# Four scheduling edits in an eight-image chain of attention layers: moments, q and k pieces, whole-width logits, and sums of the last tile on the tensor engine

## The reference

```python
def layer0(x):                       # channel attention
    q, k, v = split(W @ groupnorm32(x) + b)          # 8 heads
    a = softmax(q @ k.T * 32**-0.5)                  # 32 x 32 per head
    return x + P @ (a @ v) + pb
def layer1(x):                       # pixel attention, one head
    q, k, v = split(Wa @ x)                          # 32, 32, 128 channels
    return x + gamma * Wo @ (v @ softmax(q.T @ k).T) # 1024 x 1024
def layer2(x):                       # pixel attention, 8 heads
    q, k, v = split(W2 @ groupnorm8(x) + b2)
    return x + P2 @ (v @ softmax(q.T @ k * 32**-0.5).T) + pb2
def layer3(x):                       # the same, with the normalised x added
    n = groupnorm8(x); q, k, v = split(W3 @ n)
    return n + P3 @ (v @ softmax(q.T @ k * 32**-0.5).T) + pb3
```

## Time and profile before

| | us |
|---|---|
| median of 3 runs | 3036.81 |
| lowest, highest | 3025.49, 3037.48 |
| the profiled execution | 3033.91 |
| its span, first to last instruction | 3032.1 |

### The profile page before, as it was taken

The page is one execution under the profiler, slowest core; times in us unless marked ns, Lnnn a source line. Parts: engine busy times, 40 slices in busy tenths (PEclk is TensorE's granted clock), DMA queues, the critical chain, the costliest instruction groups (busy, mean ns, idle before and its releaser), DMA issues.

```text
span 3032.1 us, 36216 instructions
## 1 busy us (share of the span) xinstructions
PE 2834.0 (93%) x13152; PEld 1401.0 (46%) x13152; DVE 1858.0 (61%) x3293; ACT 1551.2 (51%) x2794; POOL 2178.6 (72%) x746
## 2 busy tenths in 40 slices
PE   7879999999999999999999999999999999999998
PEld 4444445544455444544445444454444544444442
DVE  1346665566756667566665666656675566767672
ACT  2214555445545555455564455544555445555554
POOL 3208787687767778677786778768777587798877
PEclk9879999999999999999999999999999999999999
DMA  2070343303433135233340334412343313433340
GB/s 83 19 95 16 44 72 58 51 19 44 85 44 54 33 46 90 31 44 57 44 86 13 43 58 71 58 28 32 54 72 58 46 23 44 72 45 44 44 58 15
DMA packets 74388, 150.87 MB, mean 50 GB/s; under 512 B 9121, under 2 KB 10657, under 8 KB 74210
## 3 DMA queue, kind: packets, MB, share of 16 engines
q1 hardware_dynamic: 74210, 148.56, 32.4%
HBM read 20.46 MB, written 16.78 MB: 12 GB/s over the span
## 4 chain that ended last, share of the span: by engine, by line
PE 63%; DMA 12%; ACT 8%; DVE 7%; POOL 6%; issue 3%; SPq 1%; ACTq 0%; POOLq 0%; DVEq 0%
PE psum L1308 15%; PE psum L1333 11%; PE psum L1277 10%; DMA Q<-lo 7%; PE psum L1252 5%; PE psum L1221 5%; PE psum L1229 4%; ACT prob L926 4%; POOL acc L822 3%; PE psum L1329 3%; DVE maxpart L1058 3%; DMA K<-hi 3%; POOL vT L822 2%; DMA Q<-max_rows 2%; PE psum L1154 2%
## 5 line engine op out<-in xcount | busy, mean ns | idle before, releaser
L1058 DVE TENSOR_REDUCE maxpart<-psum 128x1 f32<-128x512 f32 x2176 | 1411.7, 683 | 789.3 <-PE psum L1277 764.6
L926 ACT ACTIVATE prob<-psum 128x512 f32<-128x512 f32 x2176 | 1223.5, 596 | 935.0 <-PE psum L1308 888.1
L822 POOL TENSOR_TENSOR acc<-acc,prob 128x2048 f32<-128x2048 f32 (+1 forms) x322 | 1151.6, 3576 | 170.2 <-ACT prob L926 141.2
L1308 PE MATMUL psum<-Q,K 104*128 104x512 f32 x2048 | 1080.6, 529 | 94.3 <-ACT prob L926 73.5
L1277 PE MATMUL psum<-K,Q 96*128 96x512 f32 x2048 | 837.3, 411 | 32.1 <-DMA K<-hi 17.9
L1308 PEld LDWEIGHTS psum<-Q,K 104*128 104x128 f32 x2048 | 390.0, 191 | 798.8 <-ACT prob L926 487.3
L822 POOL TENSOR_TENSOR vT<-vT,prob 128x2048 f32<-128x2048 f32 x123 | 560.7, 4558 | 16.9 <-ACT prob L926 4.6
L1333 PE MATMUL psum<-prob,vT 128*32 128x512 f32 x4096 | 571.3, 618 | 0.0
L1277 PEld LDWEIGHTS psum<-K,Q 96*128 96x128 f32 x2048 | 398.3, 195 | 178.3 <-issue 89.3
L822 POOL TENSOR_TENSOR acc<-prob 128x2048 f32<-128x2048 f32 (+1 forms) x58 | 212.0, 3656 | 333.2 <-PE psum L1354 168.2
L1333 PEld LDWEIGHTS psum<-prob,vT 128*32 128x32 f32 x4096 | 99.8, 109 | 197.7 <-ACT prob L926 117.6
(11 more groups left out here) (138 smaller groups left out, 2129.2 us busy)
## 6 DMA issues: line engine op xcount, KB each, us to landing
Q<-hi SPq DMA_DIRECT2D x128, 256.0 KB
K<-hi SPq DMA_DIRECT2D x128, 256.0 KB
Q<-lo SPq DMA_DIRECT2D x64, 256.0 KB
K<-lo SPq DMA_DIRECT2D x64, 256.0 KB
scratch<-xa SPq DMA_DIRECT2D x8, 1024.0 KB, 4.0
xb<-scratch SPq DMA_DIRECT2D x8, 1024.0 KB, 4.9
xa<-in_x SPq DMA_DIRECT2D x7, 1024.0 KB, 8.4
out<-hb SPq DMA_DIRECT2D x7, 1024.0 KB, 5.7
```

Of the source, the lines that this page charges most:

```text
L822: pool.tensor_tensor(total, first if a == 1 else total, this, ALU.add).then_inc(added, 1)
L926: act.activation(prob[STEP_STARTS.slot(b, start)][:, j, :], score_bank[(SCORES.rank[b.n][e] - 1) % SCORE_BANKS], ACT.Exp, scale=1.0 if lay ...
L1058: dve.tensor_reduce(maxpart[layer][:, a // NQ, a % NQ:a % NQ + 1], bank, AX_X, ALU.max).then_inc(max_free, 1)
L1308: pe.matmul(score_bank[(r - 1) % SCORE_BANKS], left, right, start=True, stop=True).then_inc(score_full, 1)
```

## The change

Four edits.

1. "norm" loses its ACT part, which becomes an event of its own, ("moments", layer), two or three slots later. In most places "side mean" and "power" then move by one or two slots as well.
2. The q and k pieces of four heads come as q0, k0, k1, q1 where they came as q0, q1, k0, k1, at a fixed pace (every 5 slots for the early ones, every 4 for the late ones) where they were spread evenly (3.5 slots apart). The pair hi/lo is picked by (m + i) % 2, and a max product waits only for the stack that it reads. In the serial stretch of turn 0 the four v pieces are put between them.
3. The logits of four heads are one product 128 wide per half; only the blocks on the diagonal are used. DVE works on four blocks one by one, so that the maximum and the subtraction become four instructions each.
4. `pooled` takes the turn in which a group began: in turns 1 and 9, POOL leaves the last tile to PE in all groups.

```diff
-            + [("norm", layer), ("side", layer, "mean"), ("power", layer)]
+            + [("norm", layer), ("moments", layer), ("side", layer, "mean"), ("power", layer)]
...
+def place_operands(layer, t):
+    q, k = split_operand(layer, 2 * t), split_operand(layer, 2 * t + 1)
+    return q[:2] + k + q[2:]
...
+    def paced(first, step, pieces):
+        return at([first + step * i + c for i in range(len(pieces) // 2) for c in (0, 1, 1)], cut(pieces))
...
-            a += [(0, ("load",))] + at((10, 12, 14, 16, 17, 20, 23), normalise(0))
+            a += [(0, ("load",))] + at((10, 12, 14, 16, 17, 20, 22, 24), normalise(0))
...
-            a += at((1, 2, 3, 4, 5, 8, 11, 15, 16, 17, 18), normalise(3))
+            a += at((1, 2, 3, 4, 5, 8, 10, 12, 15, 16, 17, 18), normalise(3))
...
-                  + at((17, 17, 18, 18, 19, 23, 25, 28, 29, 30, 31), out1[T * NQ + 1:]),
+                  + at((17, 17, 18, 18, 19, 21, 23, 25, 28, 29, 30, 31), out1[T * NQ + 1:]),
...
-                 (3, 2, spread(1, 15, early2), [(3, 3, 8, 32, 0, 23), rows(3, 3, 27), (2, 0, 0, 8, 24, 31)]),
+                 (3, 2, paced(1, 5, early2), [(3, 3, 8, 32, 0, 23), rows(3, 3, 27), (2, 0, 0, 8, 24, 31)]),
...
-                 (2, 0, spread(0, 14, late2) + spread(SCALED, end, out3),
+                 (2, 0, paced(0, 4, late2) + spread(SCALED, end, out3),
...
-    return KC - 1 if layer != 2 and g > 0 or layer == LAST3 or (layer, g) == (2, 1) else KC
+    light = layer != 2 and g > 0 or layer == LAST3 or (layer, g) == (2, 1) or n in (1, B + 1)
+    return KC - 1 if light else KC
...
+    def split_home(m, i):
+        return (m + i) % 2
...
-                            act.wait_ge(stacked[i], b.until(STACKED[i], e))
+                            act.wait_ge(stacked[home], b.until(STACKED[home], e))
...
-                    elif e[0] == "norm":
-                        act.wait_ge(vstep, b.after(VSTEPS, e))
+                    elif e[0] == "moments":
+                        act.wait_ge(vstep, b.after(VSTEPS, ("norm", e[1])))
...
-                        own(dve.tensor_reduce(l0max[:, :], logits, AX_X, ALU.max))
+                        for r, logits in blocks:
+                            ins = dve.tensor_reduce(l0max[r, :], logits, AX_X, ALU.max)
+                        own(ins)
+                        for r, logits in blocks:
+                            ins = dve.tensor_tensor(l0[e[1]][r, :, :], logits,
+                                                    l0max[r, :].unsqueeze(2).broadcast_to([DH, T, DH]), ALU.subtract)
...
+                                ch = slice(t * P, (t + 1) * P)
+                                for k in range(T):
+                                    pe.matmul(side_bank[:, ch], wqk0_sb[:, k, ch], gk[layer][:, k, ch],
+                                              start=(k == 0), stop=False)
+                                ins = pe.matmul(side_bank[:, ch], rows0_sb[:, ch],
+                                                su_rows[layer][:, C + ch.start:C + ch.stop], start=False, stop=True)
...
-                        if a == 0 and (layer == 1 and g == 0 or layer != 1 and g % NQ == 0):
-                            ms = [0] if layer == 1 else [g // NQ * 2, g // NQ * 2 + 1]
-                            for i in range(2):
-                                pe.wait_ge(stacked[i], b.last(STACKED[i], [("stack", layer, m, i) for m in ms], e))
+                        elif g % NQ:
+                            first_use = [(m, 1)] if a == 0 else []
+                        else:
+                            first_use = {0: [(m, 0), (m + 1, 0)], 1: [(m + 1, 1)]}.get(a, [])
```

More of the change, by code:

```diff
@@ L131, in group_sequence @@
     out1 = after_layer1(False)
-    early2, late2 = (split_operand(2, m) + split_operand(2, m + 1) for m in (0, 2))
-    early3, late3 = (split_operand(3, m) + split_operand(3, m + 1) for m in (0, 2))
+    early2, late2 = (place_operands(2, t) for t in range(T))
+    early3, late3 = (place_operands(3, t) for t in range(T))
     rest0 = channel_attention(False)
@@ L170, in group_sequence @@
     early_halves, late_halves = (side(2, f"v{half}", KC // HPT) for half in range(T))
+    v2 = side(2, "v", KC // 2)
     maxima2 = [("max", 2, 0, a) for a in range(MAXIMA[2])]
@@ L441, in adds @@
         _, layer, g, s = e
+        began = n if ("score", layer, g, 0, 0) in PLANS[n][:i] else n - 1
         tiles = range(HPT * s, HPT * (s + 1)) if layer == 1 else [s]
-        return [("add", layer, g, a) for a in tiles if a and (layer == 1 or a < pooled(layer, g))]
-    ADDS = Events(PLANS, adds)
-    STACKED = [Events(PLANS, lambda e, s=s: [e] if e[0] == "stack" and e[-1] % 2 == s else [],
+        return [("add", layer, g, a) for a in tiles if a and (layer == 1 or a < pooled(began, layer, g))]
+    ADDED = [[adds(n, i, e) for i, e in enumerate(plan)] for n, plan in enumerate(PLANS)]
+    ADDS = Events([[x for of in turn for x in of] for turn in ADDED], lambda e: [e])
+    def split_home(m, i):
+        return (m + i) % 2
+    STACKED = [Events(PLANS, lambda e, s=s: [e] if e[0] == "stack" and split_home(*e[2:]) == s else [],
                       lambda e: 16 * (7 if e[1] == 1 else 3)) for s in range(2)]
@@ L695, in program @@
                         _, layer, m, i = e
-                        t, s, part = m // 2, m % 2, slice(i * QW, (i + 1) * QW)
+                        t, s, part, home = m // 2, m % 2, slice(i * QW, (i + 1) * QW), split_home(m, i)
                         low = b.after(PIECES, ("side", layer, "qk", m, i))
@@ L799, in program @@
                         slot, before = prob[VALUES.slot(b, e)], prob[VALUES.slot(b, e) - 1]
-                        for add in adds(e):
+                        for add in ADDED[b.n][b.place[e]]:
                             a = add[3]
@@ L1263, in program @@
                         half = slice((a % NQ) * QW, (a % NQ + 1) * QW)
-                        if a == 0 and (layer == 1 and g == 0 or layer != 1 and g % NQ == 0):
-                            ms = [0] if layer == 1 else [g // NQ * 2, g // NQ * 2 + 1]
-                            for i in range(2):
-                                pe.wait_ge(stacked[i], b.last(STACKED[i], [("stack", layer, m, i) for m in ms], e))
+                        m = 0 if layer == 1 else g // NQ * 2
+                        if layer == 1:
+                            first_use = [(0, a)] if g == 0 and a < NQ else []
+                        elif g % NQ:
+                            first_use = [(m, 1)] if a == 0 else []
+                        else:
+                            first_use = {0: [(m, 0), (m + 1, 0)], 1: [(m + 1, 1)]}.get(a, [])
+                        for piece in first_use:
+                            home = split_home(*piece)
+                            pe.wait_ge(stacked[home], b.last(STACKED[home], [("stack", layer) + piece], e))
                         if layer == 1:
@@ L1339, in program @@
                         _, layer, g = e
-                        add = ("add", layer, g, (KC if layer == 1 else pooled(layer, g)) - 1)
-                        at = ("values", layer, g, STEPS[1] - 1 if layer == 1 else pooled(layer, g) - 1)
-                        own = [] if layer == 1 else range(pooled(layer, g), KC)
+                        began = turn_of(b, ("score", layer, g, 0, 0), e)
+                        by_pool = KC if layer == 1 else pooled(began, layer, g)
+                        add = ("add", layer, g, by_pool - 1)
+                        at = ("values", layer, g, STEPS[1] - 1 if layer == 1 else by_pool - 1)
+                        own = [] if layer == 1 else range(by_pool, KC)
                         for tile in own:
@@ L1351, in program @@
                         pe.wait_ge(added, b.last(ADDS, [add], e, at))
-                        total = sums(sums_home(turn_of(b, ("score", layer, g, 0, 0), e), layer, g))
+                        total = sums(sums_home(began, layer, g))
                         for j in range(HPT):
```

72 lines of the change are left out of this document (32 added, 40 removed).

## The result

The changed kernel took **2931.1 us** (median of 4 runs, 2927 to 2937) against 3036.8 before (3025 to 3037). The ratio is 0.967, with a 95% interval of 0.9645 to 0.969. Timed again beside other kernels it was 0.966 (0.963 to 0.968). The profiled execution has a span of 2931.0 us against 3032.1, so 101 us are to be explained. The prediction had 77 us less, to 2957, and a range of 2920 to 3000: direction and range held.

What follows compares the result with a forecast made beforehand. PE, busy 93% of the span, was taken to set the pace. Terms 15 + 6 + 16 + 20 + 9 + 6 + 0 - 3.5 + 20 = 88.5 us, less 11 handed back, gave 77: 3033.9 to 2957 us, range 2920 to 3000.

Steps and rivals of the forecast that it cites:

- the clock: Over the 2800 us behind the opening, fewer pauses mean fewer half-clock stretches: 20 us back, some 14 of 1.4 (0 to 42).
- the hand-back: A fifth of the 57 us from the first four terms, 11 us, deducted because one ended pause lets the next appear.
- POOL's queue: In (2, 1), layer 3's "power" stands behind an add and a scaling: 0.5 us lost in each of seven turns, -3.5 us.
- the opening: Serial stretch of turn 0: v pieces fill the waits and maxima start some 6 us sooner; 6 us (0 to 9).
- Moments, 15 + 6: Later moments shorten PE's pauses: layer 2 in (3, 1), 7 x 2.2 = 15 us; layer 0 in (2, 1), 6 us.
- K wait 16: First max product, as in (2, 0), no longer waits for all four stacks, k1 in time: 16 us (12 to 17).
- hi 20: In (3, 2) and (3, 0), ACT stands less before rounding a third piece, shortening PE's pauses: 20 us (12 to 27).
- rival (c): Pieces still collide: slow stack transfers leave k1 late in (3, 2), neither wait ends; 2991 us, chance 0.07.
- the third that I had set: Sign in the profile after: ACT's waits for Q<-lo fall to a third.
- Logits, 9: In eight images, 12 wide passes take 1.6 us instead of 3.3, less longer DVE softmax: net 9 us (0 to 13).
- Last tile, 0: In turns 1 and 9, 6.3 us more PE products offset ended waits for POOL's sums: 0 us (-3 to +3).

## Why the prediction was right, and where it was not

Direction and range held, and the time was 26 us too high. That it came so near is in part luck: the clock (21 us too little), the hand-back (11) and POOL's queue (3.5) were wrong in one direction, the opening (up to 6) in the other. By the steps:

- **Moments, 15 + 6.** Undone behind the other edits 23 us, alone 9. The idle was sized fairly (24 us), by a mistake in each direction: 1.65 us in place of 2.2 in (3, 1), since a maximum of DVE was late next by 0.95 and not by 0.6, and more than 1.2 in (2, 1), where idle fell by some 2.0 us (4.1 to 2.2 in turn 1).
- **K wait 16, hi 20, opening 6.** Undone 71. The pauses were well sized (40 us of idle against 36). k1 was in time, and no K wait is left behind the opening, so rival (c) is out. ACT's wait for Q<-lo fell to far less than the third that I had set (89.3 to 1.7), but 26.1 us for K<-hi came in its place, of which PE felt some 8 us, since that much idle time goes from (3, 0) and (2, 0) when the late pieces come a slot later. What failed: I took the terms at the state of before, where longer groups hid a part of the K wait (16.6 us, 21.2 with the moments mended, 26.1 with all else mended), and I put the lapses into a separate, small term.
- **Opening, 6.** Not confirmed: no difference can be told between the orders, with 6 us inside the uncertainty. What I had said of the mechanism is half right: the maxima start sooner, and a wait for the third stack and for DVE takes most of it back.
- **Logits, 9.** The total is right, 7 to 9, in part by luck. Twelve wide passes took 2.1 us and not 1.6, and the narrow ones brought lapses that the sum did not have. PE waits 0.6 us for the longer softmax, as said.
- **Last tile, 0.** Too low: 5 by the trace, 9 by the time. The waits for POOL's sums would have grown to 12.0 us in all.
- **POOL's queue, -3.5.** It cost nothing. The gvar that power needs comes as the scaling ends, and ACT has no wait for gb. From turn 6 of after:

```profile
1490.73 1.28 POOL L811 TENSOR_TENSOR att<-att,turned_sums 128x512 f32<-128x512 f32 x1 [0.88 <-DVE turned_sums L1108]
1492.28 0.70 POOL L788 TENSOR_TENSOR rstd<-gvar,half_power 128x2 f32<-128x2 f32 x1 [0.27 <-DVE gvar L1017]
...
1494.36 0.80 ACT L863 ACTIVATE hb<-xb,gb,ga 128x512 f32<-128x512 f32 x1
```

- **Clock, 20.** This is the term that was mis-sized most. It is up to 41: the 88 us that were not granted became 47. I counted 14 lapses of 1.4 us. Behind the opening they went from 24 to 5 (8 in the second profile of the same kernel), and they cost 1.4 us each where they were short and 2.3 to 2.8 where they were long. My sentence that lapses begin right behind pauses of one us or more also goes too far: of the 24 in the kernel before, two follow pauses of about half a us only, among them the longest, and two the narrow logits.
- **The hand-back, 11.** As a mechanism it is real (the maximum's 0.95, and 14 of the moments' 23 us when they are mended alone). As a discount on the whole it was wrong: once nearly all pauses in a turn are mended, nothing is left to take the lapse.

Together: 55 us less idle and 46 less busy. Of the latter the logits are 11, the last tile is -6, and the rest is 41, as much as the clock gave back. The split is rough, since PE's busy time in a group also moved by 0.8 us at an unchanged full grant.

How pauses and lapses go together, over the stretch from 230 us to 50 us before the end of each profile. The pauses are those of PE of one us or more in the time line, the lapses the stretches at 1.2 GHz in the clock's own record:

| kernel | pauses of 1 us or more | lapses | profiled span, us |
|---|---|---|---|
| before | 30 | 24 | 3032 |
| moments alone | 20 | 20 | 3018 |
| pieces undone | 15 | 17 | 3006 |
| moments undone | 15 | 13 | 2958 |
| one wait for all stacks | 11 | 13 | 2990 |
| last tile undone | 8 | 11 | 2946 |
| pieces evenly spread | 9 | 9 | 2957 |
| logits undone | 5 | 10 | 2939 |
| late pieces a slot later, attv moved | 6 | 2 | 2932 |
| after, two profiles | 3, 3 | 5, 8 | 2931, 2930 |
| opening undone | 3 | 4 | 2926 |
| late pieces a slot later, stats spread | 7 | 9 | 2926 |
| late pieces a slot later | 0 | 5 | 2919 |

This is a correlation over kernels, with exceptions. Most lapses go down with the pauses, and the experiment that puts one pause back puts lapses back in its very group. But the six pauses of 1.59 us with attv moved had no lapse behind them, and the five lapses of the last row follow pauses of 0.60 to 0.79 us. Why a lapse comes in one place and not in the other stays open, also why one pause of 2.65 us is followed by none.

## What to carry to other kernels

Where PE is the bound at over 90%, count a pause as its length, and add a lapse of up to 2 to 3 us as a chance and not as a rule: read its price from pairs of equal groups at different grants, and how often it comes from the clock's record. Look at several pairs, since lapses have more than one length. Look also at runs of narrow passes, which were followed by lapses without any pause. Take the worth of an edit in the state that the others leave: a wait for a transfer or for a slower engine grows as the work in front of it shrinks, so one edit alone gave 9 us where it was worth 23 at the end, and one that looked free was worth some 5 to 9. And where transfers of several pieces feed one consumer, wait for each at its first use before you spread them out: the same order and pace without that cost 60 us.

## What I had not expected of the hardware

- A lapse of TensorE's clock costs as much as a long pause: 2.3 us behind one of 2.65, and 2.8 behind one of 4.7 (group grants of 0.92 in place of 1.00), 1.4 us at a grant of 0.96.
- It is not bound to a given pause. The same 2.65 us in the same group went with a longer group at a lower grant in turns 3, 4 and 6 to 8, and with a full grant in turn 5. Six pauses of 1.59 us had none behind them, and pauses of 0.6 us sometimes did.
- Narrow fp32 passes were followed by a lapse while PE never stood still, in nine of eighteen turns (5.50 us busy of 5.50 at 1.00, then 6.50 of 6.50 at 0.50).
- 48 passes of 128x32 into four column tiles took 3.4 us, against 2.1 for 12 of 128x128. A head's narrow passes cost 0.41 us; a wide pass cost 0.17 in the mean.
